# The four Gelus of a batch in one run on ScalarE, with three PSUM banks for the first MLP product

## What is computed

```python
x = L0_attn_x                                        # (8, 512, 128): 8 batches of 512 tokens
h = _layernorm(x) * (1 + ca) + sa
x = x + ga * _L0_attn_ref(h, ...)
h = _layernorm(x) * (1 + cb) + sb
x = x + gb * _L0_ffn_ref(h, Wg, Wu, Wd)              # 8 experts: silu(x @ wg) * (x @ wu) @ wd
h = _layernorm(x) * (1 + ca) + sa
x = x + ga * _L1_attn_ref(h, Wqkv, Wout, ...)        # 8 heads, causal softmax
h = _layernorm(x) * (1 + cb) + sb
x = x + gb * _L1_ffn_ref(h, Wq, Wk, Wv, Ws, Wd, Wo)  # 16 heads, softmax, top-2 of 8 values per head

def _L0_attn_ref(x, ...):
    ...                                              # linear attention, 16 heads, then:
    x = x + attn_out
    h = layer_norm(x, norm2_g, norm2_b)
    h = jax.nn.gelu(jnp.einsum('bnc,hc->bnh', h, fc1_w) + fc1_b, approximate=False)
    h = jnp.einsum('bnh,ch->bnc', h, fc2_w) + fc2_b
    return x + h
```

## Time and profile before

| what | value |
|---|---|
| median of three runs | 3120.25 us (3118.91 to 3121.88) |
| the profiled execution, its own time | 3122.04 us |
| its span, first to last instruction | 3120.1 us |
| mean granted clock of TensorE | 0.911 of full speed |
| TensorE busy | 2548.0 us (82%) |
| VectorE busy | 1751.7 us (56%) |
| ScalarE busy | 1613.9 us (52%) |
| GpSimd busy | 788.4 us (25%) |
| table loads ahead of Gelu | 20 of 1283 ns |

### The profile page before, as it was taken

How to read it: one execution, slowest core, us unless ns; L and a number is a source line. 1 busy time by engine, 2 the same in 40 slices (tenths; PEclk the granted TensorE clock), 3 DMA queues, 4 the chain that set the end, 5 groups by cost and what they waited for, 6 DMA issues and landing times.

```text
span 3120.1 us, 44672 instructions
## 1 busy us (share of the span) xinstructions
PE 2548.0 (82%) x14892; PEld 1689.8 (54%) x14892; DVE 1751.7 (56%) x2906; ACT 1613.9 (52%) x3329; POOL 788.4 (25%) x370
## 2 busy tenths in 40 slices
PE   3984698789797997889787897979979797996487
PEld 2453347664476545765376644765457553774265
DVE  4235763547645494465935567364854649447732
ACT  0241246663566636664366635666366643774474
POOL 1003520106401181013601055011810127004500
PEclk7996799999898998999999998999989999998698
DMA  2110010102001120012101020011200121001001
GB/s 73 47 41 8 10 51 1 55 14 76 12 15 41 41 59 2 15 55 55 32 1 47 22 65 22 9 48 41 59 2 15 48 55 38 15 15 39 0 28 31
DMA packets 210739, 101.63 MB, mean 33 GB/s; under 512 B 137367, under 2 KB 189620, under 8 KB 210492
## 3 DMA queue, kind: packets, MB, share of 16 engines
q1 hardware_dynamic: 205052, 95.74, 11.1%
q10 hardware_dynamic: 5440, 2.75, 0.3%
HBM read 77.48 MB, written 20.99 MB: 32 GB/s over the span
## 4 chain that ended last, share of the span: by engine, by line
PE 61%; DVE 14%; issue 14%; ACT 8%; POOL 2%; DMA 1%; DVEq 0%; ACTq 0%; POOLq 0%; SPq 0%
PE bank L719 9%; PE bank L834 6%; PE bank L1016 6%; PE bank L831 6%; PE bank L839 6%; PE bank L871 5%; PE bank L979 4%; PE bank L887 4%; PE bank L980 3%; DVE vals L1495 2%; PE bank L997 2%; ACT pr L1202 2%; DVE prod L1487 2%; DVE nrm_o L1304 2%; DVE nmax L1529 1%
## 5 line engine op out<-in xcount | busy, mean ns | idle before, releaser
L704 POOL TENSOR_TENSOR prod<-pv,mixv 128x1024 f32<-128x1024 f32 x184 | 589.8, 3234 | 305.4 <-ACT pv L1141 157.1
L1529 DVE TENSOR_REDUCE nmax<-bank 128x1 f32<-128x512 f32 x512 | 351.0, 690 | 539.9 <-PE bank L980 519.3
L1202 ACT ACTIVATE pr<-bank,nmax 128x512 f32<-128x512 f32 x512 | 350.7, 685 | 189.3 <-DVE nmax L1529 187.6
L1180 ACT ACTIVATE prT<-bank 128x512 f32<-128x512 f32 x512 | 305.0, 596 | 258.0 <-PE bank L719 251.8
L643 POOL TENSOR_TENSOR rstd<-vareps,minus_half 128x4 f32<-128x4 f32 x48 | 50.0, 1043 | 1495.5 <-DVE vareps L1299 1495.4
L1083 ACT ACTIVATE arena<-bank 128x512 f32<-128x512 f32 x256 | 152.8, 597 | 444.3 <-PE bank L831 397.3
L979 PE MATMUL bank<-keys,q_high 128*128 128x512 f32 x512 | 267.6, 523 | 113.3 <-DVE on L1544 30.9
L719 PE MATMUL bank<-ident,pr 128*128 128x128 f32 x2048 | 327.1, 284 | 29.0 <-ACT prT L1180 28.6
L719 PEld LDWEIGHTS bank<-ident,pr 128*128 128x128 f32 x2048 | 256.9, 146 | 118.8 <-ACT prT L1180 41.9
L1495 DVE TENSOR_REDUCE vals<-prod 128x128 f32<-128x1024 f32 x256 | 306.9, 1209 | 11.7 <-POOL prod L704 10.8
L834 PE MATMUL bank<-h1T,Wu 128*128 128x512 f32 x512 | 272.1, 614 | 40.0 <-DVE arena L1389 39.9
(11 more groups left out here) (226 smaller groups left out, 3878.0 us busy)
## 6 DMA issues: line engine op xcount, KB each, us to landing
Wg<-in_L_ffn_Wg SPq DMA_DIRECT2D x64, 256.0 KB, 2.9
Wu<-in_L_ffn_Wu SPq DMA_DIRECT2D x64, 256.0 KB, 3.5
Wd<-in_L_ffn_Wd SPq DMA_DIRECT2D x64, 256.0 KB, 3.9
out_rows<-on SPq DMA_DIRECT2D x32, 512.0 KB, 2.6
onR<-out_rows SPq DMA_DIRECT2D x32, 512.0 KB, 3.9
xin<-in_L_attn_x SPq DMA_DIRECT2D x8, 256.0 KB, 4.3
mask_rows<-masko SPq DMA_DIRECT2D x8, 256.0 KB, 4.6
maskR<-mask_rows SPq DMA_DIRECT2D x8, 256.0 KB, 6.6
```

The lines of the kernel that those rows point to most:

```text
L704: g.tensor_tensor(*value_piece(n), ALU.mult).then_inc(vprod_r[0], 1)
L1202: s.activation(pr[:, x % 2, :], bank_k[:, :], ACT.Exp, bias=nmax[:, x % 2:x % 2 + 1], accum_out=den[:, i % 2, h:h + 1]).then_inc(s_out[0], 1)
L1529: v.tensor_reduce(nmax[:, m % 2:m % 2 + 1], (S0, S1)[turn % 2][:, :], X_AXIS, ALU.max, negate=True).then_inc(nmax_r[0], 1)
```

## The change

TensorE issues fc1[0], fc1[1] and fc1[2] together at mark 17, the third into bank F0. fc1[3] moves to mark 19 and waits for the first Gelu. fc2[0] and fc2[1] stand at mark 20, fc2[2] and fc2[3] at mark 21. ScalarE has all four Gelus at mark 19, one behind the other. The output is complete at mark 21 as before, and VectorE's reader at mark 22 is unchanged.

```diff
--- before.py
+++ after.py
@@ -793,16 +793,16 @@
                 ln_turn(b, 2, F1)
                 yield 16
                 wait(pe, ln_evac, b, 2)
-                for j in range(NJ + 1):
-                    if j < NJ:
-                        if j >= 2:
-                            wait(pe, hid_r, b, j - 1)
-                        pe.matmul((F2, F3)[j % 2][:, :], fc1T[:, j * P:(j + 1) * P], h2T[:, :], start=True, stop=True).then_inc(fc1_ps[0], 1)
-                    if j >= 1:
-                        wait(pe, hid_r, b, j)
-                        last = pe.matmul(F1[:, :], fc2T[:, j - 1, :], hid[:, j - 1, :], start=(j == 1), stop=(j == NJ))
-                    if j < NJ:
-                        yield 17 + j
+                for j in range(NJ):
+                    if j == 3:
+                        yield 18
+                        wait(pe, hid_r, b, 1)
+                    pe.matmul((F2, F3, F0)[j % 3][:, :], fc1T[:, j * P:(j + 1) * P], h2T[:, :], start=True, stop=True).then_inc(fc1_ps[0], 1)
+                for j in range(NJ):
+                    if j % 2 == 0:
+                        yield 19 + j // 2
+                    wait(pe, hid_r, b, j + 1)
+                    last = pe.matmul(F1[:, :], fc2T[:, j, :], hid[:, j, :], start=(j == 0), stop=(j == NJ - 1))
                 last.then_inc(fc2_ps[0], 1)
                 yield 22
                 wait(pe, y0_r, b, 1)
@@ -1062,11 +1062,10 @@
                 s.activation(attT[:, :], F1[:, :], ACT.Copy).then_inc(attT0_r[0], 1)
                 yield 15
                 ln_out(b, 2, h1T[:, :], F1[:, :], cols[:, 2:3], cols[:, 3:4])
-                yield 16
+                yield 18
                 for j in range(NJ):
                     wait(s, fc1_ps, b, j + 1)
-                    s.activation(hid[:, j, :], (F2, F3)[j % 2][:, :], ACT.Gelu, bias=cols[:, 4 + j:5 + j]).then_inc(hid_r[0], 1)
-                    yield 17 + j
+                    s.activation(hid[:, j, :], (F2, F3, F0)[j % 3][:, :], ACT.Gelu, bias=cols[:, 4 + j:5 + j]).then_inc(hid_r[0], 1)
                 yield 24
 
             def moe_in(b):
```

## The result

The changed kernel takes 3148.82 us (median of six runs, 3140.77 to 3155.40) beside 3121.07 us for the kernel before (six runs, 3118.91 to 3128.11): ratio 1.0077, 95% interval 1.0060 to 1.0095. A second measurement gave 1.0076 (1.0061 to 1.0091). So the change makes the kernel slower by some 24 us; on the 3120.25 us from which the prediction started that is 3144 us, where the forecast said 3135 and 3120 to 3146. The profiled execution, at 3140.82 us with a span of 3137.7, is one of the quicker ones.

What follows compares the result with a forecast made beforehand. TensorE was taken as the bound, with ScalarE close to full in the stretch. 3122.0 + 8.1 (delay) + 6.8 (clock) = 3137 us on the profiled execution, 3135 us for the median; range 3120 to 3146.

Steps and rivals of the forecast that it cites:

- The wait: TensorE ahead of fc1[3], batches 2 to 7: idle 2.38 us until the first Gelu, behind the Exp of head 56.
- The delay per batch: Scores of head 58 start 1.35 us later in each of six batches, kept to the end: +8.1 us.
- The clock: TensorE's granted clock falls behind the new wait in four of six batches, 1.7 us each: +6.8 us.
- The relative: Similar TensorE wait in the experts' stage, 2.07 to 2.12 us at six places, four with a clock fall.
- Batch 1: Batches 0 and 1, without Exp beside them: no load goes, 0 taken, up to -1.5 us for both.
- The forecast's own mechanism: Net wait of 1.0 to 1.7 us per batch and zero to six clock falls: 64%, 3126 to 3141.
- the third rival: Clock falls twice as long at each of the six places, 20.5 us: 3149 us, 12%.
- The first: Rival: ScalarE is the bound and loads the gain, all three TensorE waits go: 3108 us, 10%.
- The decision point: At fc1[3]: whether the first Gelu is done when TensorE arrives at 671.82, needing Exp of head 56 by 668.98.
- The second: Rival: delay made good behind the stretch, or stall half as long, no clock loss: 3120 us, 12%.

Runs made afterwards that it cites:

- e0: The changed kernel, unaltered, run again for its spread: 3147.27 us, ratio 1.0076 to the kernel before.
- e8: Changed kernel with fc1[3] and the Gelus one mark earlier in batches 0 and 1, ahead of the copy of keys: 3143.37 us, ratio 1.0063.
- e6: Changed kernel with two banks, fc1[0] and fc1[1] at mark 17, fc1[2] and fc1[3] behind the wait at mark 19: 3148.58 us, ratio 1.0070.
- e9: Changed kernel with two unused filler products in the wait of fc1[3] (batches 2 to 7) and batches 0 and 1's Gelus one mark earlier: 3139.33 us, ratio 1.0053.
- e2: Changed kernel with fc1[3] one mark later, behind the mixed products and transposes of head 55: 3130.34 us, ratio 1.0015.
- e3: Changed kernel with all four first products at mark 17 into four banks: 3129.46 us, ratio 1.0023.
- e4: Changed kernel with Identity in place of Gelu, so no table load among the heads: ratio 1.0017.
- e5: Kernel before with Identity in place of Gelu, so all six loads per batch go: ratio 0.9986.
- e7: Changed kernel with four banks, first products in pairs at marks 17 and 18, four Gelus at mark 18, one head earlier: 3119.14 us, ratio 0.9983.

## Why the prediction was right, and where it fell short

**Direction and mechanism: right.** The chain was read as it came. Set against fc1[0], the scores of head 56 were forecast at +4.98 us (669.68 - 664.70) and came at 674.15 - 669.17 = 4.98; the value products ahead of the wait at +6.09 and 6.08; the end of the wait at +9.50 and 9.51. The wait was forecast as 2.38 us from the end of the value products; 678.68 - (675.25 + 1.02) gives 2.41. The delay per batch was forecast as 1.35 and is 1.26: the work behind the wait takes 688.03 - 678.68 = 9.35 us where 9.45 was counted. It stands to the end as argued: from the maximum of head 58 to the first Silu it is 16.3 us with the clock up, before and after. So 6 x 1.26 = 7.6 us of the 8.1 (7.5 by the maxima).

**The clock: right in kind, the size by chance.** Four falls of six at 1.7 us were taken from the experts' stage. A fall costs 1.58 us. Their number is 0, 3 and 2 of six in the three traces of this order of batches 2 to 7 (changed, e0, e8) and 4 in e6; on average some two, 3 us and not 6.8. The relative was no steady measure either: at its six places the clock fell 4, 4 and 3 times in the three traces of the kernel before, but 0 times in the changed kernel's and 2 in e0's. Some more of it lies just behind the stretch: from the maximum of head 58 to the first Silu the six batches take 99.4, 99.8 and 100.7 us in these traces, against 98.6, 98.0 and 98.1 before, 1.7 us.

**Batch 1: the step that was mis-sized.** "No Exp stands beside them, so no load goes", and "0 taken", looked only at TensorE's waits for Gelus in batch 0. It left out that ScalarE's queue was moved past a copy of `values` that waits for TensorE, in a place with TensorE at half clock for the first 5 us. Price: 31.84 and 35.73 against 29.3 us, +4.4 us on average, and e8 takes it away.

**The sum, by the traces.** The mean span of the changed kernel's two traces is 3140.4, of the kernel before's three 3123.5: 16.9 us. The stretches give (118.3 + 122.8) / 2 - 110.8 = 9.7, the part behind them 1.4, batch 1 4.4: 15.5 us together. The ratios of the timed runs say 24 us (19 to 30). Of the other 8 us no part was taken into the forecast, and no run shows their cause. e9 shows the same: its span is 9.0 us above the mean of before, of which 7.5 is the stretch, but its timed runs are 16.6 us above. A like remainder, some 2 to 9 us, is left in all the other kernels of the table but e2 when the three parts are taken from the ratio, also where the long wait is gone (e3, e4, e5, e7); so that wait is not what makes it. What does stays open. The traces point to one place: the six stretches from the maximum of head 32 to fc1[0], which nothing in the change touches, sum to 410.4, 412.8 and 410.5 us in the three traces of before and to 414.2 on average in the eleven other traces (409.5 to 417.0), at more time on the lower clock. That the new length of a batch shifts the moments of these falls is a guess; no run separated it.

**The range.** That it holds is in part luck. The forecast's own mechanism was given 3126 to 3141, and the 3144 on its scale lies above that, in the part of the range that stood for the third rival, which was not seen; what filled it was batch 1 and the 8 us that stay open.

**Rivals.** The first (ScalarE the bound, 3108 us) did not happen: fc1[3] found its bank taken and the time rose. Its price was too high as well: e5 removed the loads outright, the stretches fell by the 11.9 us that it counted, and the time by 4.4 (0 to 9). The decision point that it named was the right one: e7 brings the first Gelu to where TensorE wants it and the waits go. The second (made good behind) did not happen, by the 16.3 us above; the third (the fall twice as long) was seen in no stretch of batches 2 to 7.

## What to carry to other kernels

Grouping activations by table saves time on ScalarE, and it also moves the first result of the group to the place of the last; ask which engine's next instruction needs that first result, and what is queued behind it. Here a run of four Gelus with two loads per batch made the kernel some 24 us slower in one place and some 5 us faster one head earlier (e7), with a fourth bank and with the waiting products put where their operands were ready. Where such a run is moved, follow it through every stage that it is interleaved with: the six alike batches were costed to 0.1 us each, and the one that differed cost more than half as much as all of them.

## What was not expected of the hardware

A wait of 2.33 us, the same to the hundredth in all batches, had 3.4 us at 1.2 GHz at its end in 9 of 24 cases and none there in 15; with the wait cut to 0.42 us or less by products of no use, 0 of 12 had it. The mean granted clock of an execution goes with its time, if loosely: of 63 timed executions of the kernel before, the ten quickest (3114.8 to 3120.0 us) had 0.911 of full speed on average and the ten slowest (3129.4 to 3134.8 us) 0.906, with the kernel unchanged. A few us on a kernel of this length are therefore known only from many runs.
